# A state-space stage by halves of the tokens, with its convolution on TensorE

## What is computed

```python
x = x + cross_and_self_attention(layernorm(x), ctx)      # fp8-rounded projection at its end
x = x + state_space(layernorm(x))                        # the change is here
x = x + experts(layernorm(x))                            # 8 experts, top 2 of a router
x = x + read_memory(layernorm(x), ctx, mask)
x = x + rotary_attention(layernorm(x))
x = x + ffn_from_table(layernorm(x))

def state_space(x):                                      # (8, 32, 256)
    xc    = causal_conv(x, conv_w, 4 taps) + conv_b      # each channel by itself
    B, C, dt = split(x @ Wxproj.T)                       # 64 each
    delta = softplus(dt);  dA = exp(-exp(A_log) * delta)
    Bu    = delta * B * (xc @ Winproj.T)
    h     = scan(h_t = dA_t * h_{t-1} + Bu_t)
    return (C * h) @ Woutproj.T + D * xc
```

## Time and profile before

| | us |
|---|---|
| median of 3 runs | 469.26 |
| lowest and highest | 468.91, 471.06 |
| the profiled execution, its own time | 467.07 |
| its span, first to last instruction | 465.6 |
| PE busy | 427.6 (92%) |
| DVE busy | 362.8 (78%) |
| ACT busy | 261.0 (56%) |
| POOL busy | 26.5 (6%) |
| state-space stage and next norm, L1396 to the first expert product | 349.23 to 367.80 |

### The profile page before, as it was taken

How to read it: one execution, slowest core, us unless ns; L and a number is a source line. 1 busy time by engine, 2 the same in 40 slices (tenths; PEclk the granted TensorE clock), 3 DMA queues, 4 the chain that set the end, 5 groups by cost and what they waited for, 6 DMA issues and landing times.

```text
span 465.6 us, 6890 instructions
## 1 busy us (share of the span) xinstructions
PE 427.6 (92%) x2421; PEld 298.5 (64%) x2424; DVE 362.8 (78%) x761; ACT 261.0 (56%) x808; POOL 26.5 (6%) x33
## 2 busy tenths in 40 slices
PE   5988899989999999999999999999897899977687
PEld 2443445667887675758767676776584699926376
DVE  5888695848799869689799998976968799567741
ACT  1465889998552777866987677484103173221250
POOL 0000000000030000100001000200100022000000
PEclk9999999999999999999999999999989899999899
DMA  8258020223301104684843834795457778430000
GB/s 294 115 208 334 0 91 0 89 96 126 124 0 41 51 1 118 134 284 98 181 113 68 200 76 85 168 270 202 93 115 266 284 270 209 86 114 1 2 1 23
DMA packets 14047, 58.57 MB, mean 126 GB/s; under 512 B 1792, under 2 KB 2496, under 8 KB 12480
## 3 DMA queue, kind: packets, MB, share of 16 engines
q1 hardware_dynamic: 10992, 41.66, 24.5%
q0 software_dynamic: 3024, 16.52, 18.1%
HBM read 41.40 MB, written 0.26 MB: 89 GB/s over the span
## 4 chain that ended last, share of the span: by engine, by line
PE 73%; ACT 11%; DVE 11%; issue 2%; DMA 2%; SPq 0%; DVEq 0%; ACTq 0%
PE PS L458 12%; PE PS L431 9%; PE PS L433 8%; PE PS L432 8%; PE PS L1733 3%; PE PS L1096 3%; ACT raw_dt.float L1865 3%; PE PS L1762 2%; PE PS L1229 2%; PE PS L505 2%; PE PS L478 2%; ACT raw_dt.float L1845 2%; ACT sq_dt.float L578 2%; PE PS L1078 2%; PE PS L467 1%
## 5 line engine op out<-in xcount | busy, mean ns | idle before, releaser
L578 ACT ACTIVATE sq_dt.float<-PS 128x128 bf16<-128x128 f32 x256 | 67.3, 281 | 28.9 <-PE PS L433 22.3
L458 PE MATMUL PS<-s_dt.float,ctx_ring_dt.float 128*128 128x512 f32 x128 | 57.7, 593 | 1.3 <-DVE px_dt.float L812 1.3
L431 PE MATMUL PS<-wkc_dt.float32r,ctx_hi_dt.float32r 128*128 128x512 f32 x128 | 53.6, 419 | 1.7 <-ACT sq_dt.float L578 1.2
L578 ACT ACTIVATION_READ_ACCUMULATOR sq_dt.float<-PS 128x1 f32 x256 | 53.8, 211 | 0.0
L433 PE MATMUL PS<-wkc_dt.float32r,ctxT_ring_dt.float32r 128*128 128x512 f32 x128 | 50.3, 393 | 0.0
L432 PE MATMUL PS<-wkT_dt.float32r,ctx_hi_dt.float32r 128*128 128x512 f32 x128 | 50.1, 392 | 0.0
L1733 PE MATMUL PS<-wch_dt.float,xs_dt.float 128*128 128x512 f32 x96 | 42.2, 594 | 0.7 <-DVE xs_dt.float L1968 0.7
L655 ACT ACTIVATE luttmp_dt.float<-low_bit_dt.float,vec_dt.float,small_dt.float 128x1536 f32<-128x1536 uint8 x24 | 38.5, 1654 | 2.0 <-DMA lutw_dt.float<-luttmp_dt.float 2.0
L458 PEld LDWEIGHTS PS<-s_dt.float,ctx_ring_dt.float 128*128 128x128 f32 x128 | 23.6, 190 | 25.0 <-issue 23.0
L662 DVE SCALAR_TENSOR_TENSOR luttmp_dt.float<-idx_dt.float,luttmp_dt.float 128x1536 f32<-128x1536 uint8 x21 | 36.4, 1750 | 0.0
L431 PEld LDWEIGHTS PS<-wkc_dt.float32r,ctx_hi_dt.float32r 128*128 128x128 f32 x128 | 24.0, 187 | 14.1 <-ACT sq_dt.float L578 9.2
(11 more groups left out here) (296 smaller groups left out, 882.2 us busy)
## 6 DMA issues: line engine op xcount, KB each, us to landing
lutw_dt.float<-luttmp_dt.float POOLq DMA_DIRECT2D x21, 768.0 KB, 6.5
wch_dt.float<-in_chunks SPq DMA_DIRECT2D x6, 1024.0 KB, 5.0
ctxT_ring_dt.float<-in_ctxT SPq DMA_DIRECT2D x8, 512.0 KB, 4.0
ctx_ring_dt.float<-in_ctx SPq DMA_DIRECT2D x8, 512.0 KB, 3.4
keysT_dt.float<-in_ctxT SPq DMA_DIRECT2D x8, 512.0 KB, 7.4
keys_dt.float<-in_ctx SPq DMA_DIRECT2D x8, 512.0 KB, 7.9
luttmp_dt.float<-in_idx SPq DMA_DIRECT2D x3, 768.0 KB, 6.4
zu_dt.float<-in_wproj SPq DMA_DIRECT2D x1, 2048.0 KB, 7.2
```

Of the source, the lines that this page charges most:

```text
L431: nc.tensor.matmul(o, x_hi, hi[:, c, :], start=c == 0, stop=False)
L458: last = nc.tensor.matmul(bank(5 + c), keysr[k][:, t, c * 128:c * 128 + 128], sS[k][:, t, :], start=t == 0, stop=t == KT - 1)
L578: last = nc.scalar.activation(sq[:, (4 * hf + g) * D:(4 * hf + g + 1) * D], bank(hf)[:, g * D:(g + 1) * D], ACT.Square, accum_out=ssq[:, k ...
```

## The change

The stage is cut into two halves of 128 tokens. The convolution moves from VectorE to TensorE: for each tap and channel group a 128x128 diagonal matrix (`convw`) is the stationary operand and the shifted `hpad` the moving one, and four products sum up in PSUM. ScalarE writes the 8 matrices in the last loop step, into the place of the context ring, and later reads the sums with the bias into `xc`. ScalarE also copies the transposes into `hpad`. The norm of this stage and of the next go by halves with `half_stats` and `half_normal`, the routing products and the split of `hT` too. The idle products become 4, 5 and 3 instead of 14 and 11. The exponential of `a_log` moves into the loop step. Other lines only count their semaphores anew.

```diff
-    ("A_last", NH * C, FRONT, LOOP), ("ctxT_ring", 2 * CT * NK, FRONT, LAST), ("ctx_ring", 2 * KT * C, FRONT, LAST),
+    ("A_last", NH * C, FRONT, LOOP), ("ctxT_ring", 2 * CT * NK, FRONT, LOOP), ("ctx_ring", 2 * KT * C, FRONT, LAST),
+    ("convw", 4 * CT * 128, LAST, LAST, "ctxT_ring"),
...
             step(7, 1, more=False, next_context=False)
+            act.wait_ge(st_full, 4 * B)
+            for k in range(4):
+                for c in range(CT):
+                    nc.scalar.activation(convw[:, k * CT + c, :], const("ident"), ACT.Copy,
+                                         scale=col("conv_w", 4 * c + k)).then_inc(taps_ready, 1)
             inverse(7)
+            self_step(nc.scalar.activation(negA[0:SSM, :], col("a_log")[0:SSM, :], ACT.Exp))
+            self_step(nc.scalar.activation(negA[0:SSM, :], negA[0:SSM, :], ACT.Copy, scale=-1.0))
...
         def tail_pe(pe):
+            def convolve(j):
+                pe.wait_ge(hT_ready, 1 + j)
+                pe.wait_ge(taps_ready, 4 * CT)
+                for c in range(CT):
+                    for k in range(4):
+                        last = nc.tensor.matmul(bank(SSM_X[j], CT, 128)[:, c, :], convw[:, k * CT + c, :],
+                                                hpad[:, c, 4 * j:4 * j + 4, k:S + k], start=k == 0, stop=k == 3)
+                last.then_inc(conv_full, 1)
...
-            keep_clock(14, 7)
-            turn_norm(1, (1, 6))
...
+            keep_clock(4, 2)
+            turn_half(1, 0)
             pe.wait_ge(ld_w["ssm"], 48)
...
+            ssm_inputs(0)
+            convolve(0)
+            turn_half(1, 1)
+            ssm_states(0)
+            convolve(1)
+            ssm_inputs(1)
             pe.wait_ge(diag_d, 1)
...
+            ssm_skip(0)
+            ssm_outputs(0)
+            ssm_states(1)
+            ssm_skip(1)
+            ssm_outputs(1)
+            keep_clock(5, 4)
+            turn_half(2, 0)
+            route(0)
+            turn_half(2, 1)
+            route(1)
+            keep_clock(3, 4)
...
-            pe.wait_ge(hT_split, 1)
+            pe.wait_ge(hT_split, 2)
...
         def tail_act(act, step):
+            def pad_half(j):
+                act.wait_ge(turned, 1 + j)
+                act.wait_ge(hpad_zero, 1)
+                nc.scalar.activation(hpad[:, :, 4 * j:4 * j + 4, 3:S + 3],
+                                     bank(TURNED[1, j], CT, 4, S), ACT.Copy).then_inc(hT_ready, 1)
+
+            def read_conv(j):
+                act.wait_ge(conv_full, 1 + j)
+                for c in range(CT):
+                    last = nc.scalar.activation(xc[:, c, 128 * j:128 * j + 128], bank(SSM_X[j], CT, 128)[:, c, :],
+                                                ACT.Identity, bias=col("conv_b", c))
+                last.then_inc(conv_ready, 1)
...
+            half_rstd(1, 0)
             act.wait_ge(loop_over, 3)
...
+            pad_half(0)
+            half_rstd(1, 1)
+            softplus(0)
+            pad_half(1)
+            read_conv(0)
+            decays(0)
+            read_conv(1)
+            softplus(1)
+            decays(1)
...
+            half_rstd(2, 0)
             hi_of_experts(0)
+            half_rstd(2, 1)
+            hi_of_tokens(0)
+            hi_of_tokens(1)
             hi_of_experts(1)
...
         def tail_dve(dve, step):
+            dve.wait_ge(loop_over, 3)
+            half_stats(1, 0)
+            half_normal(1, 0)
             dve.wait_ge(proj_out, 2)
             nc.vector.scalar_tensor_tensor(x[:, 1, :], bank(1)[:, 0:C], pscale, x[:, 1, :], ALU.mult, ALU.add)\
                 .then_inc(x_ready, 1)
-
-            norm(1)
...
-            for k in range(1, 4):
-                for c in range(CT):
-                    last = nc.vector.scalar_tensor_tensor(xcv[:, c], hpad[:, c, :, k:S + k], col("conv_w", 4 * c + k),
-                                                          xcv[:, c], ALU.mult, ALU.add)
...
+            half_stats(1, 1)
+            half_normal(1, 1)
+            step_sizes(0)
+            scan(0)
+            step_sizes(1)
+            add_ssm(0)
+            half_stats(2, 0)
+            scan(1)
+            half_normal(2, 0)
+            add_ssm(1)
+            half_stats(2, 1)
+            read_half(2, 0)
+            half_normal(2, 1)
...
+            lo_of_tokens(0)
             lo_of_experts(0)
-            dve.wait_ge(ssm_out_full, 1)
-            nc.vector.tensor_tensor(x, x, bank(5, TT, C), ALU.add).then_inc(x_ready, 1)
...
+            read_half(2, 1)
+            lo_of_tokens(1)
             lo_of_experts(1)
-            dve.wait_ge(route_full, 1)
+            dve.wait_ge(route_full, 2)
```

230 lines of the change are left out of this document (103 added, 127 removed).

## The result

| | before | changed |
|---|---|---|
| median of 20 runs each, same set | 471.18 us (466.20 to 473.78) | 475.1 us (469.88 to 478.29) |
| ratio | | 1.0072, interval 1.0044 to 1.0099 |
| span of the profiled execution | 465.6 | 476.8 |
| mean granted clock of TensorE | 0.989 | 0.968 |

The changed kernel is slower by 0.7% of 471.18, 3.4 us, with 2.1 to 4.7 us by the interval. Executions more than 1.5% above the fastest of their kernel count as slow and are left out of every ratio, though not of the medians: here four of the changed kernel's 20, the profiled one among them, which is why the medians are 3.9 us apart. The forecast was +2.8 us, which lies inside the interval; the time forecast was 472.1 in a range of 469.4 to 474.4, and 475.1 lies outside.

A forecast was written before the change was run, and what follows sets the result against it. The stage was taken as bound by VectorE's chain, the experts by TensorE. The add of half 0 comes 1.2 us earlier, VectorE then needs 4.2 more, 0.15 was slack: +2.8 us, median 472.1 us, range 469.4 to 474.4.

The forecast's parts named there:

- The base: Whole kernel: the profiled execution lies 2.2 us below the median of 469.26, so the changed median should be 472.1 us.
- The taps cost nothing: ScalarE before the inverse at 331.73: 8 matrix writes, at most 2.8 us, fit into 5.41 us of free time.
- Step 1: TensorE up to the output of half 0: the add of half 0 starts at 360.4, only 1.2 us earlier.
- The stated bound for the spacing: TensorE's short products in the stage: spacing between 0.109 and 0.125 us, worth -0.2 to +0.9 us over 64 instructions.
- Step 2: VectorE's queue from the add of half 0 to the experts: first expert product at 370.1 in place of 367.8.
- the weights' low part slips into a wait: VectorE before the experts: the 1.22 us and the second high part hidden again, +0.5 to +2, 470.5 us; chance 0.17.
- From the second low part to the down product: Routing through VectorE's product, behind the second expert's low part: unchanged, so the down product is released at 378.0, not 375.15.
- A low clock there costs nothing until 0.5 us are used up: TensorE's expert products: done at 377.45, then waiting for the down product at 378.0, so a low clock has 0.5 us slack.
- TensorE's clock falls inside the stage: Stage up to the experts' start: low clock costs up to 1.7 us, or 0.5 to 2 later; 474 us; chance 0.12.
- three signs named as proof against the forecast: Changed profile: add of half 0 before 358.5, weights' low part costing nothing, or TensorE reaching the down product last.
- TensorE no longer waits for VectorE: Stage: the convolution's 3.5 us leave the path and the halves overlap, about -3 us, 466.3 us; chance 0.08.
- products run closer: TensorE's 128-column fp32 products: at three quarters of 0.11 us, step 1 is 1.8 us shorter, +1.0, 470.3 us; chance 0.03.

The follow-up runs named there:

- after_again: The changed kernel, same code, run and profiled once more beside the kernel before: median 474.75 us, ratio 1.0085.
- best2_bare: Changed kernel with TensorE's, ScalarE's and VectorE's work reordered, first two experts' weight parts made earlier, no idle products behind the last skip product: 470.77 us, 0.9980 of before.
- nofill: The changed kernel without its 12 idle products of the stage: median 474.17 us, ratio 1.0040 to the kernel before.
- fill: The changed kernel with 25 idle products instead of 8 behind the last skip product: median 473.29 us, ratio 1.0077 to the kernel before.
- whole_pe: The kernel before with only the convolution moved to TensorE by tap matrices, over all 256 tokens, no halves: median 474.78 us, ratio 1.0120.
- best: Changed kernel with first two experts' weight parts early, half 1's transposes before half 0's convolution, its inputs behind half 0's output, 26 idle products: 470.51 us, 1.0011 of before.

## Why the prediction was wrong in its time and right in its reasons

- **The base.** The step that failed is "That execution lies 2.2 us below the median of 469.26, so the median should be 472.1 us". The median of the kernel before in the result's own set is 471.18, 1.9 us higher, and 469.82, 470.84, 471.15 and 471.35 in the other sets; 469.26 is the median of three runs, which stood low. With 471.18 the same sum of +2.8 gives 474.0, inside the range, which allowed "some 0.5" for the spread of medians. The other 1.1 us to 475.1 are in the cost: 3.9 us between these medians, 3.4 us by the ratio (2.1 to 4.7), where the sum had 2.8. The next points say which terms were too small.
- **The taps cost nothing:** right. 2.44 us for at most 2.8, the inverse not delayed.
- **Step 1:** the add of half 0 was due at 11.2 and came at 11.6 in both profiles. From the states of half 0 to that add TensorE needed 5.4 us in place of 4.8: the convolution took 1.98 for 1.8 (16 instructions, 0.124 each, where 0.112 was taken), the inputs 1.45 for 1.3, and the states and the skip term about 0.6 each for 0.45. The states started 0.2 us sooner than reckoned. The stated bound for the spacing, 0.125, held for the convolution and the inputs.
- **Step 2:** right in `after_again` to 0.2 us at each landmark. The first expert's low part starts 18.3 behind half 1 of `x` (forecast 18.2) and is uncovered, so the rival "the weights' low part slips into a wait" fell; the second's starts at 21.2 (21.4). In `best2_bare` both lie in an earlier wait and delay nothing.
- **From the second low part to the down product:** "Routing, exponential, table load, `silu` and VectorE's product are unchanged behind it". They took 8.1 us in place of 7.5, because one instruction took 1.02 us in place of 0.43; see the last section.
- **The clock.** "A low clock there costs nothing until 0.5 us are used up" held in `after_again`, where TensorE was done first. It failed in the first profile: the clock fell at 366.4, not at the experts' start, and went through products that were on the way: 2.25 us for five idle ones, 1.29 for three, and TensorE reached the down product last. That is the rival "TensorE's clock falls inside the stage", with 1.9 us more than in `after_again`, and one of the three signs named as proof against the forecast. How often it happens in this kernel is open, since that profile is of its slowest execution. The idle products were not counted as a cost behind the output; `nofill`, whose down product comes 0.8 us sooner, points to one.
- **The rival "TensorE no longer waits for VectorE"** fell as argued: the order has the second convolution ahead of the output, and the add of half 1, the one that ends the stage, went from 12.4 to 15.3.
- **The rival "products run closer"** fell: 0.124 us. The Trainium skill (TensorE: Matmul & The Clock Gate, Back-to-back issue gap) has about 81 ns for each matmul of a 128-column stream; the trace has half as much again for these fp32 instructions.

## What to carry to other kernels

Moving work from a busy engine to an idle one gains only if the two engines did not already work side by side: here TensorE's inputs and VectorE's convolution overlapped before, and in a row they put the add 2.8 us later. Cutting a stage into halves pays when the last half's chain gets shorter, so cost the chain of half 1 and not the first result; and every operation that fitted into a wait of the old order needs a new wait of its own. Before an engine is made faster, ask what its signals release: in `fill` and `whole_pe` earlier expert products started GpSimd's mask in the middle of VectorE's routing. Take the base from as many runs as can be had, and allow for its spread before a range is given.

## What the runs showed that was not expected

The granted clock fell in stretches in which TensorE was far from idle: 2.00 us of work in 3.40 us ahead of 366.4, and with 25 idle products in the gaps (`fill`) it stayed at 1.00 to 375.0 and fell then. What a low clock costs hangs on who is last at the first down product. That is VectorE in `after_again`, `fill`, `best` and `whole_pe`, and TensorE in the other profiles, by 0.2 us in `before` and by 0.9 in `best2_bare` (VectorE's product ends at 373.71, the down product starts at 374.62). With 0.50 for 3.4 us there, `best2_bare` still has the shortest way to the down product of all the altered kernels.

VectorE's clamp of 128x512 in fp32 took 0.41 to 0.43 us in most cases and 1.02 to 1.30 in others, and each slow one began when GpSimd was already at work on the mask. In `after_again` the GpSimd row is

```profile
378.13 1.04 POOL L1438 CAST mask_dt.float<-maskraw_dt.float 128x1024 f32<-128x1024 uint8 x1 [33.14 <-PE PS L1120]
```

beside the clamp at 378.44 that took 1.02 us (above). In `best`, clamp and mask started together, VectorE's row first:

```profile
375.32 1.30 DVE L1549 TENSOR_SCALAR moe_dt.float<-moe_dt.float 128x512 f32<-128x512 f32 x1 [0.71 <-ACT moe_dt.float L1370]
```

```profile
375.30 1.04 POOL L1442 CAST mask_dt.float<-maskraw_dt.float 128x1024 f32<-128x1024 uint8 x1 [31.13 <-PE PS L1124]
```

and in the first profile of the changed kernel, where the mask came behind it, VectorE's row and GpSimd's:

```profile
381.43 0.43 DVE L1545 TENSOR_SCALAR moe_dt.float<-moe_dt.float 128x512 f32<-128x512 f32 x1 [0.71 <-ACT moe_dt.float L1366]
```

```profile
382.30 1.04 POOL L1438 CAST mask_dt.float<-maskraw_dt.float 128x1024 f32<-128x1024 uint8 x1 [36.12 <-PE PS L1120]
```

In the kernel before the clamp began at 373.85 and the mask at 373.94: the clamp took 0.43 us and the mask's first step 1.25 in place of 1.04. The mask stands 0.09 us behind the clamp there, 0.31 ahead in `after_again`, 0.87 behind in the first profile, so it does not start with it: its program waits for the third group of expert products (`gu_full` 3), that is for TensorE, and a moved clamp can meet it or miss it. In `fill` and `whole_pe` it met small steps of the routing instead, each a TENSOR_TENSOR, which has two operands. These ended when GpSimd's step did, within 0.03 us in all four cases: 374.27 and 375.42 beside 374.26 and 375.40 in `fill`, 374.38 and 375.52 beside 374.35 and 375.50 in `whole_pe`. The slow clamps of `after_again` and `best` ended 0.3 us behind it. So the rows say that VectorE's instruction was held until GpSimd's was over, rather than slowed throughout; no run took the mask away, which would be the test.
